# An audio-tower layer pair on one core: plain gathers with additions for six token tiles, adding gathers for six, and the causal mask written into PSUM by TensorE

## The chip, the cores and the metric

The kernel runs on one core of a Trainium2 chip. The metric is the device time of one execution in microseconds (us). The kernel before took 1510.72 us, the median of 3 runs (1509.34 to 1511.55). All times in the rows are us from the start of one profiled execution.

## The reference

64 sequences of 23 tokens (1472 tokens, 12 tiles of 128) pass through a token embedding and two layers:

```python
x -> tok:    layer_norm, x @ W, layer_norm                       # 1024 -> 512
L0 attention: power attention, 8 heads, gated                    # a = (q.k)**2 * exp(gate)
L0 ffn:      16 experts, top 4 of each token, plus a shared one  # h += sum of 4 expert rows
L1 attention: layer_norm, q (16 heads of 32), k, v (4 groups)
              rope, s = q.k / sqrt(32), causal softmax within each sequence, @ v, @ Wo, + h
L1 ffn:      quantized bit-linear feed-forward, + h
```

The change lies between the end of the L0 feed-forward and the end of the L1 attention.

## The kernel before

The program is written by hand for each engine, with semaphores between them; each engine runs its own list in order, so the order of the lists is the schedule. `h` holds the residual rows of all 12 tiles in SBUF.

The experts work on 61 tiles of slots. A token's row goes to four slots, and each slot's result is written to `yslot` in HBM (`keep`). When all are written, the four result rows of each token are added to `h`: `share(k, j)` (L502) is an indirect DMA issued by GpSimd that gathers, for the 128 tokens of tile `k`, the `j`-th row from `yslot` and adds it to `h` in flight. Each of the four of a tile waits by a semaphore until the one before it has landed. `shares(g, j)` issues the three of a group of three tiles. There are 48 in all. While the first run, TensorE still computes the last six tiles of the shared expert, whose result VectorE adds to `h` (L1738). Then VectorE and ScalarE prepare the weights of the next layer (`unit_a_lo`, `unit_b_lo`, L1395).

The L1 attention works in four chunks `c` of 16 sequences (368 tokens), which are not tile borders: chunk `c` needs the normalized tiles up to group `c` (three tiles each). For a group, VectorE takes statistics (`group_stats`, L1413, L1420), GpSimd the inverse root (`turned_root`, L466), VectorE the shift (`group_shift`, L1427); ScalarE normalizes (`normed`), TensorE turns the rows (`row_turn_l1`, L924), ScalarE and VectorE split the result into two half-precision parts (`high` L611, `low` L1432).

For a chunk, TensorE projects five blocks of queries and keys and one of values (`project`), into two PSUM banks in turn; ScalarE moves each out (`moved`, L786). VectorE shuffles (`rotate`, L1830), and the products with cosine and sine are shared out between VectorE (L1835) and GpSimd (`cosine`, L539, L541). VectorE sums them to `kr` and `qp` (`rotated`, L1844, L1845). TensorE forms the scores in PSUM banks 2 to 5 (L1255, 64 matmuls of float32, which the trace shows as 128). `centred` (L1848) is three passes of VectorE over 1472 columns: scores plus mask from PSUM into SBUF (L1852), row maximum (L1857), subtraction (L1858). After the first of them the banks are free (`f_cp`). ScalarE takes the exponential (L790), VectorE sums and scales (`weights`, L1864 to L1870), TensorE turns the weights (`turn`, L1265) and multiplies by the values (`weighted`, L1282, which writes the same banks 2 to 5), and ScalarE and VectorE split the result (`y_high` L803, `y_low` L1877). The turns of the rows for the next chunk stand between the projections in chunks 0 and 2, and after the weighted sums in chunk 1. The output projection and the second feed-forward follow (first row added at L1915).

## Time and profile before

| | |
|---|---|
| profiled execution | 1511.43 us, span 1509.5 us |
| TensorE busy | 1294.1 us (86%) |
| VectorE busy | 896.4 us (59%) |
| ScalarE busy | 629.5 us (42%) |
| GpSimd busy | 308.6 us (20%) |
| adding gathers (L506) | 48, mean 1684 ns, busy 80.8 us |
| chain of waits by line | L506 3%, L1255 2%, L539 1% of the span |

Busy shares are means over the whole span. In the stretch that the change touches no engine is full for long: GpSimd is, at first, and then the engines wait for each other in turn. A row of the timeline gives the start, the duration, engine, line and operation, and in brackets how long the engine sat idle before it and which instruction ended the wait; "issue" is time in which it waited for nothing that the profile shows.

### The profile page before, as it was taken

To read this page: it belongs to the slowest core of one execution; us is meant where nothing else is said; L and a number is where in the kernel's file an instruction comes from. 1 tells how busy PE (TensorE), PEld (TensorE's weight loads), DVE (VectorE), ACT (ScalarE), POOL (GpSimd) and SP (SyncE) were. 2 spreads that over 40 slices of the span, in tenths; PEclk is the share of its full clock that TensorE was granted. 3 is DMA by queue.
4 is the path that set the end of the run, shared out by engine and by line. 5 is a ranking of instruction groups with operands and counts; after the bars stand their busy time and mean duration, and the time that the engine had idled before them with its cause. 6 is when DMAs were issued, how large, how long until landed. Compare 5 with 4: busy or idle time off the path is not lost.

```text
span 1509.5 us, 30358 instructions
## 1 busy us (share of the span) xinstructions
PE 1294.1 (86%) x10660; PEld 829.6 (55%) x10674; DVE 896.4 (59%) x1865; ACT 629.5 (42%) x1066; POOL 308.6 (20%) x336
## 2 busy tenths in 40 slices
PE   6878899999999999986759999999972868768997
PEld 3446677777777877764424444444531656424443
DVE  5776455555565555668653555544332665578886
ACT  3445344444444444442314444444431333236664
POOL 2443000000000000000012233333267853010000
PEclk9997999999999999996779999999995869789999
DMA  5111343524435352422315767865268520000000
GB/s 181 68 66 43 100 178 138 200 105 174 142 127 204 135 185 109 156 85 89 124 70 178 257 227 257 303 242 170 98 125 133 85 43 3 2 1 8 21 21 32
DMA packets 44238, 184.26 MB, mean 122 GB/s; under 512 B 8688, under 2 KB 9200, under 8 KB 36368
## 3 DMA queue, kind: packets, MB, share of 16 engines
q0 software_dynamic: 21280, 95.41, 20.3%
q1 hardware_dynamic: 19440, 75.41, 14.3%
q10 hardware_dynamic: 3456, 12.58, 2.3%
q8 instruction: 42, 0.69, 0.2%
q14 instruction: 20, 0.16, 0.0%
HBM read 135.65 MB, written 47.73 MB: 121 GB/s over the span
## 4 chain that ended last, share of the span: by engine, by line
PE 55%; DVE 18%; issue 13%; POOL 7%; ACT 4%; DMA 2%; DVEq 1%; ACTq 0%; POOLq 0%; SPq 0%
PE ps L929 14%; PE ps L931 13%; PE ps L930 13%; POOL h L506 3%; PE ps L1036 3%; PE ps L1019 3%; PE ps L1255 2%; DVE ff L1976 2%; DVE amf L1983 1%; PE ps L1120 1%; PE ps L1052 1%; POOL rt_out L466 1%; PE ps L1348 1%; PE ps L1366 1%; POOL qraw L539 1%
## 5 line engine op out<-in xcount | busy, mean ns | idle before, releaser
L929 PE MATMUL ps<-nT_hi,wa_hi 128*128 128x368 f16 x448 | 147.9, 330 | 11.8 <-DVE wa_lo L1395 8.1
L930 PE MATMUL ps<-nT_lo,wa_hi 128*128 128x368 f16 x448 | 147.3, 329 | 0.0
L931 PE MATMUL ps<-nT_hi,wa_lo 128*128 128x368 f16 x448 | 147.0, 328 | 0.1
L496 POOL DMA_INDIRECT xg<-xrow,idx x61 | 61.4, 1007 | 276.7 <-PE ps L1120 121.5
L1559 DVE TENSOR_TENSOR a<-sq,E 92x368 f32<-92x368 f32 x64 | 31.7, 534 | 136.3 <-ACT sq L694 136.3
L1731 DVE SCALAR_TENSOR_TENSOR nrm<-ps,xg,nrm 128x256 f32<-128x256 f32 x61 | 29.5, 484 | 133.3 <-ACT nrm L737 112.1
L930 PE MATMUL ps<-wa_lo,nT_hi 128*92 128x128 f16 (+1 forms) x560 | 107.1, 235 | 0.0
L929 PE MATMUL ps<-wa_hi,nT_hi 128*92 128x128 f16 (+1 forms) x560 | 107.1, 235 | 0.0
L931 PE MATMUL ps<-wa_hi,nT_lo 128*92 128x128 f16 (+1 forms) x560 | 107.1, 235 | 0.0
L929 PE MATMUL ps<-wide,xT 128*128 x244 | 93.6, 383 | 12.9 <-issue 8.2
L491 POOL DMA_DIRECT2D wsp<-we_sp x16 | 8.6, 539 | 446.6 <-DVE we_sp L1395 446.6
L706 ACT ACTIVATE yT_hi<-ps 128x368 f16<-128x368 f32 x64 | 27.9, 475 | 164.9 <-PE ps L1052 164.9
L930 PE MATMUL ps<-wide,xT 128*128 x244 | 93.2, 382 | 0.0
L931 PE MATMUL ps<-wide,xT 128*128 x244 | 93.2, 382 | 0.0
L1533 DVE SCALAR_TENSOR_TENSOR wide<-ps,wide 128x368 f32<-128x368 f32 x128 | 69.1, 540 | 40.1 <-PE ps L931 40.1
L1348 PE MATMUL ps<-qw,qT 128*128 128x512 bf16 x372 | 86.5, 386 | 3.9 <-DVE ff L1976 2.6
L506 POOL DMA_INDIRECT h<-yslot,slot x48 | 80.8, 1684 | 15.4 <-issue 13.1
L929 PE MATMUL ps<-yT_hi,wb_hi 128*128 128x368 f16 x256 | 82.9, 324 | 1.2 <-DVE yT_lo L1581 1.2
L930 PE MATMUL ps<-yT_lo,wb_hi 128*128 128x368 f16 x256 | 82.8, 324 | 0.0
L931 PE MATMUL ps<-yT_hi,wb_lo 128*128 128x368 f16 x256 | 82.8, 324 | 0.0
L668 ACT ACTIVATE qk<-ps 128x368 f32<-128x368 f32 x96 | 45.1, 479 | 84.6 <-PE ps L931 84.5
L728 ACT ACTIVATE xT<-ps 128x1024 f16<-128x1024 f16 x61 | 62.3, 1022 | 28.9 <-PE ps L1120 22.0
(302 smaller groups left out, 3326.1 us busy)
## 6 DMA issues: line engine op xcount, KB each, us to landing
we_st<-in_we POOLq DMA_DIRECT2D x16, 1536.0 KB, 6.8
wsp<-we_sp POOLq DMA_DIRECT2D x16, 1536.0 KB, 5.4
wide<-wsp SPq DMA_DIRECT2D x16, 1536.0 KB
yslot<-yt POOLq DMA_DIRECT2D x61, 256.0 KB
wq_st<-in_ffq SPq DMA_DIRECT2D x24, 512.0 KB, 6.0
wq_st<-in_ffq ACTq DMA_DIRECT2D x24, 512.0 KB
wide<-in_wa SPq DMA_DIRECT2D x10, 1024.0 KB, 4.8
xt<-in_x SPq DMA_DIRECT2D x12, 512.0 KB, 3.5
```

The costliest lines, as they stand in the source:

```text
L496: pool.indirect_dma_start(Q["xg"][:, g % 4, :].bitcast(U32), None, xrow, bass.IndirectOffsetOnAxis(ap=idx[:, g:g + 1], axis=0)).then_inc(x ...
L506: pool.indirect_dma_start(h[:, k, :], None, yslot, bass.IndirectOffsetOnAxis(ap=slot[:, k, j:j + 1], axis=0), compute_op=ALU.add).then_inc ...
L668: nc.scalar.activation(B["qk"][:, j, :], ps[:, j % 2, 0:CW], ACT.Copy, scale=1.0 / WS).then_inc(b_ev, 1)
L728: nc.scalar.activation(Q["xT"][:, p].rearrange("p a b -> p (a b)"), ps[:, p, :].bitcast(F16), ACT.Copy).then_inc(m_xe, 1)
L929: nc.tensor.matmul(dst, lhs[0], rhs[0], start=start, stop=False)
L930: nc.tensor.matmul(dst, lhs[0], rhs[1], start=False, stop=False)
L931: return nc.tensor.matmul(dst, lhs[1], rhs[0], start=False, stop=stop)
L1019: ins = nc.tensor.matmul(ps[0:AT, 2 + j, a * REP * AT:(a + 1) * REP * AT], B["qk"][:, 2, tok], B["qk"][:, 0:2, tok], start=True, stop=True)
L1036: ins = nc.tensor.matmul(ps[0:AT, 4 + 2 * j + a, r * (DH + 1):(r + 1) * (DH + 1)], B["a"][0:AT, j, a, r, :], B["v1"][0:AT, 2 * j + a, :], ...
L1348: ins = nc.tensor.matmul(ps[:, 2 * (f % 2) + q, :], Gm["qT"][:, b, ds(k * P, P)], qw[:, q, b * FF + f * 512:b * FF + (f + 1) * 512], start ...
L1533: V.scalar_tensor_tensor(acc, ps[:, 6 + blk % 2, 0:CW], 1.0 / (WS * AS), acc, ALU.mult, ALU.add).then_inc(b_acc, 1)
L1559: V.tensor_tensor(B["a"][0:AT, j], B["sq"][0:AT, j], B["E"][0:AT, 2 * j:2 * j + 2].unsqueeze(2).broadcast_to([AT, 2, REP, AT]), ALU.mult). ...
```

## The change

Tiles 0 to 5 no longer use adding gathers. `collect(k)` issues four plain gathers into a landing buffer (three in the space of the expert weights, one in `wq_st`; tiles 4 and 5 reuse the buffers of tiles 0 and 1 and wait until these are read). VectorE adds the four rows and `h` with four additions (`returned`) ahead of the tile's statistics. Tiles 6 to 11 keep their adding gathers, at other places of GpSimd's list.

The mask becomes a bfloat16 tile `maskb` for 16 sequences. TensorE writes it into each of the four PSUM banks with one matmul by the identity, and the scores accumulate onto it. `centred` then has two passes, both reading PSUM: maximum and subtraction. The banks are free only after the subtraction (`f_sb`).

The order of the chunks is written alike for all: the turns of the next chunk's rows stand behind the scores, in chunk 0 ahead of them; the statistics of group `c + 1` stand behind the sums of chunk `c`; in chunks 1 to 3 the sine product of block 3 goes from GpSimd to VectorE.

```diff
+            def collect(k):
+                if k > 3:
+                    pool.wait_ge(c_h, ready(NT + k - 4))
+                for j in range(TOPK):
+                    pool.indirect_dma_start(landing[k][:, j, :], None, yslot,
+                                            bass.IndirectOffsetOnAxis(ap=slot[:, k, j:j + 1], axis=0)).then_inc(sh_in[k], 16)
...
-                if c and j < 4:
+                if c and j < 3:
                     nc.gpsimd.tensor_tensor(Fm["qs"][:, j, :], Fm["qs"][:, j, :], sinT[:], ALU.mult).then_inc(f_cos, 1)
-            for j in range(TOPK):
-                shares(0, j)
-                shares(1, j)
+            for k in range(5):
+                collect(k)
+            turned_root(0)
+            collect(5)
...
+            turned_root(2)
+            shares(3, 0)
+            shares(3, 1)
+            cosine(2, 0)
+            cosine(2, 1)
+            shares(3, 2)
+            cosine(2, 2)
+            shares(3, 3)
+            cosine(2, 3)
+            cosine(2, 4)
+            turned_root(3)
...
@@ TensorE, scores @@
+                for g in range(G4):
+                    nc.tensor.matmul(ps[:, 2 + g, 0:CW], identb[:], maskb[:], start=True, stop=False)
...
-                                               Fm["kr"][d, s * SL:(s + 1) * SL], start=True, stop=True)
+                                               Fm["kr"][d, s * SL:(s + 1) * SL], start=False, stop=s == 15)
@@ TensorE, weighted @@
-                    pe.wait_ge(f_cp, c + 2)
+                    pe.wait_ge(f_sb, c + 2)
@@ TensorE, chunks @@
                 for j in range(2, 6):
                     project(c, j)
-                    if c % 2 == 0 and j < 5:
-                        row_turn_l1(k + j - 2)
                 if c:
                     turn(c - 1)
+                    scores(c)
+                    weighted(c - 1)
+                if c + 1 < CH:
+                    for j in range(GT):
+                        row_turn_l1(k + j)
                 if c == 0:
+                    scores(c)
+                if c + 1 < CH:
                     project(c + 1, 0)
                     project(c + 1, 1)
...
@@ VectorE @@
+            def returned(k):
+                y = landing[k]
+                dve.wait_ge(sh_in[k], SHARES[k] + 64)
+                dve.sem_inc(passed, 1)
+                V.tensor_tensor(y[:, 0, :], y[:, 0, :], y[:, 1, :], ALU.add)
+                order(V.tensor_tensor(y[:, 2, :], y[:, 2, :], y[:, 3, :], ALU.add))
+                order(V.tensor_tensor(row(k), row(k), y[:, 0, :], ALU.add))
+                V.tensor_tensor(row(k), row(k), y[:, 2, :], ALU.add).then_inc(c_h, 1)
...
+            V.tensor_copy(maskb[:].rearrange("p (h s) -> p h s", s=SL), mask1[:].unsqueeze(1).broadcast_to([P, 16, SL])).then_inc(f_mk, 1)
             group_stats(0)
             group_shift(0)
-            group_stats(1)
...
+            rotate(0, 0)
+            rotate(0, 1)
+            group_stats(1)
+            dve.wait_ge(wa_hi, UNITS + 1)
+            split_lo(wo[1][:].rearrange("p a b -> p (a b)"), st_a[:], wo[0][:].rearrange("p a b -> p (a b)"), wa_lo)
             for c in range(CH):
                 k = GT * (c + 1)
-                rotate(c, 0)
-                rotate(c, 1)
                 if c:
+                    rotate(c, 0)
+                    rotate(c, 1)
                     weights(c - 1)
                 for j in range(2, 5):
-                    if c % 2 == 0:
-                        low(k + j - 2)
                     rotate(c, j)
+                if c == 0:
+                    group_shift(1)
                 rotated(c)
...
+                if 0 < c < CH - 1:
+                    group_stats(c + 1)
+                    group_shift(c + 1)
                 if c:
+                    centred(c)
                     y_low(c - 1)
-                if c == 1:
+                if c + 1 < CH:
                     for j in range(GT):
                         low(k + j)
```

GpSimd, from the last write of the expert results to the first roots of the attention, before (`h<-yslot` is an adding gather of one tile, `rt_out` the root of one group):

```order
L500 DMA yslot<-yt 128x512 x6
L506 DMA h<-yslot,slot 128x512 x27
L466 TENSOR_TENSOR rt_out<-rt_in,neg_half 128x3
L549 MEMSET qp 128x64x9
L506 DMA h<-yslot,slot 128x512 x3
L466 TENSOR_TENSOR rt_out<-rt_in,neg_half 128x3
```

The same place in the changed kernel (`wide<-yslot` and `wq_st<-yslot` are plain gathers into landing buffers):

```order
L504 DMA yslot<-yt 128x512 x6
L510 DMA wide<-yslot,slot 128x512 x12
L510 DMA wq_st<-yslot,slot 128x512 x4
L510 DMA wide<-yslot,slot 128x512 x4
L470 TENSOR_TENSOR rt_out<-rt_in,neg_half 128x3
L510 DMA wide<-yslot,slot 128x512 x4
L516 DMA h<-yslot,slot 128x512 x3
L549 TENSOR_TENSOR qraw<-qraw,cosT 128x368 x2
L561 MEMSET qp 128x64x9
```

Thirty adding gathers stood ahead of the root of group 1 and 27 ahead of that of group 0; now 20 plain ones stand ahead of the root of group 0, and the adding gathers of group 2 begin behind it.

GpSimd at chunk 2, before (the root at the end of the first three lines is that of group 3, the products are those of chunk 2's five blocks):

```order
L506 DMA h<-yslot,slot 128x512 x3
L466 TENSOR_TENSOR rt_out<-rt_in,neg_half 128x3
L506 DMA h<-yslot,slot 128x512 x3
L466 TENSOR_TENSOR rt_out<-rt_in,neg_half 128x3
L539 TENSOR_TENSOR qraw<-qraw,cosT 128x368
L541 TENSOR_TENSOR qs<-qs,sinT 128x368
L539 TENSOR_TENSOR qraw<-qraw,cosT 128x368
L541 TENSOR_TENSOR qs<-qs,sinT 128x368
L539 TENSOR_TENSOR qraw<-qraw,cosT 128x368
L541 TENSOR_TENSOR qs<-qs,sinT 128x368
```

The same place in the changed kernel:

```order
L516 DMA h<-yslot,slot 128x512 x6
L549 TENSOR_TENSOR qraw<-qraw,cosT 128x368
L551 TENSOR_TENSOR qs<-qs,sinT 128x368
L549 TENSOR_TENSOR qraw<-qraw,cosT 128x368
L551 TENSOR_TENSOR qs<-qs,sinT 128x368
L516 DMA h<-yslot,slot 128x512 x3
L549 TENSOR_TENSOR qraw<-qraw,cosT 128x368
L551 TENSOR_TENSOR qs<-qs,sinT 128x368
L516 DMA h<-yslot,slot 128x512 x3
L549 TENSOR_TENSOR qraw<-qraw,cosT 128x368 x2
L470 TENSOR_TENSOR rt_out<-rt_in,neg_half 128x3
```

Before, all gathers were out ahead of chunk 2's products; now six of them stand between these products.

VectorE, from the centring of chunk 2 to the first shuffles of chunk 3, before:

```order
L1852 TENSOR_TENSOR wide<-ps,mask 128x1472
L1857 TENSOR_REDUCE mx<-wide 128x64
L1858 TENSOR_TENSOR wide<-wide,mx 128x1472
L1877 TENSOR_TENSOR nT_lo<-ps,nT_hi 128x4x4x23 x4
L1830 STREAM_SHUFFLE qs<-qraw 128x368 x2
```

The same place in the changed kernel:

```order
L1868 TENSOR_REDUCE mx<-ps 128x64
L1869 TENSOR_TENSOR wide<-ps,mx 128x1472
L1889 TENSOR_TENSOR nT_lo<-ps,nT_hi 128x4x4x23 x4
L1432 TENSOR_TENSOR nT_lo<-ps,nT_hi 128x4x128 x3
L1844 STREAM_SHUFFLE qs<-qraw 128x368 x2
```

A pass of the centring is gone, and the three low halves of the next chunk's rows (`L1432`) stand between the centring and chunk 3; before, they stood between the shuffles of chunk 2.

TensorE after the scores of chunk 2, before (only the first of the projection's matmuls are shown):

```order
L1265 MATMUL ps<-ident,wide 128x128 x16
L1255 MATMUL ps<-kr,qp 128x23 x64
L929 MATMUL ps<-nT_hi,wa_hi 128x368
L930 MATMUL ps<-nT_lo,wa_hi 128x368
L931 MATMUL ps<-nT_hi,wa_lo 128x368
```

The same place in the changed kernel:

```order
L1270 MATMUL ps<-ident,wide 128x128 x16
L1256 MATMUL ps<-maskb,identb 128x368 x4
L1260 MATMUL ps<-kr,qp 128x23 x64
L1287 MATMUL ps<-wide,V 32x92 x64
L925 MATMUL ps<-ident,nrm 128x128 x12
L930 MATMUL ps<-nT_hi,wa_hi 128x368
```

The weighted sums and the twelve matmuls that turn three row tiles now stand between the scores and the first projection of chunk 3.

## Rows read from the trace of the kernel before

**Rows 1.** Busy time by stage; columns: us, then each engine busy (instructions), PEclk, DMA share, GB/s.

```profile
1104.00:1158.00 54.00, 18.81 (x101) 8.74 (x99) 14.25 (x27) 9.86 (x17) 45.57 (x29) 0.73 0.89 147
...
1308.00:1509.50 201.50, 172.84 (x933) 82.54 (x944) 162.48 (x360) 101.75 (x205) 16.39 (x26) 0.96 0.04 15
```

**Rows 2.** GpSimd in order of time, plain gather: start us, us, engine line op.

```profile
787.84 0.95 POOL L496 DMA_INDIRECT xg<-xrow,idx  x1 [0.30 <-issue]
```

**Rows 3.** GpSimd in order of time, around the adding gathers.

```profile
1138.13 1.55 POOL L506 DMA_INDIRECT h<-yslot,slot  x1 [0.30 <-issue]
...
1168.32 0.96 POOL L539 TENSOR_TENSOR qraw<-qraw,cosT 128x368 f32<-128x368 f32 x1 [4.05 <-DVE qs L1830]
...
1241.66 0.96 POOL L541 TENSOR_TENSOR qs<-qs,sinT 128x368 f32<-128x368 f32 x1
```

**Rows 4.** VectorE in order of time, shared tiles to the first shift.

```profile
1104.94 0.68 DVE L1738 SCALAR_TENSOR_TENSOR h<-ps,h 128x512 f32<-128x512 f32 x1
...
1127.07 1.22 DVE L1395 SCALAR_TENSOR_TENSOR wb_lo<-wide,wb_hi 128x1024 f16<-128x1024 f32 x1
...
1145.61 0.70 DVE L1413 BATCH_NORM_STATS2 bst<-h 128x6 f32<-128x512 f32 x1 [17.33 <-issue]
...
1157.29 0.16 DVE L1427 SCALAR_TENSOR_TENSOR nb<-mv,rt_out 128x3 f32<-128x3 f32 x1 [6.51 <-POOL rt_out L466]
```

**Rows 5.** VectorE in order of time: root answered, ordered successor, products, output weights.

```profile
1167.67 0.57 DVE L1830 STREAM_SHUFFLE qs<-qraw 128x368 f32<-128x368 f32 x1
...
1168.39 1.28 DVE L1835 TENSOR_TENSOR qs<-qs,sinT 128x368 f32<-128x368 f32 x1 [0.15 <-DVE qs L1830]
...
1186.61 2.29 DVE L1395 SCALAR_TENSOR_TENSOR wo_lo<-wide,wo_hi 128x2048 f16<-128x2048 f32 x1
...
1236.24 0.16 DVE L1427 SCALAR_TENSOR_TENSOR nb<-mv,rt_out 128x3 f32<-128x3 f32 x1 [0.99 <-POOL rt_out L466]
...
1311.50 0.18 DVE L1922 BATCH_NORM_AGGREGATE mv<-bst 128x2 f32<-128x6 f32 x1 [0.15 <-DVE bst L1920]
```

**Rows 6.** VectorE in order of time: chunk starts, centring ends, stage end.

```profile
1198.93 0.56 DVE L1830 STREAM_SHUFFLE qs<-qraw 128x368 f32<-128x368 f32 x1
...
1237.50 0.57 DVE L1830 STREAM_SHUFFLE qs<-qraw 128x368 f32<-128x368 f32 x1
...
1261.53 1.69 DVE L1858 TENSOR_TENSOR wide<-wide,mx 128x1472 f32<-128x1472 f32 x1
...
1293.54 1.89 DVE L1877 TENSOR_TENSOR nT_lo<-ps,nT_hi 128x368 f16<-128x368 f32 x4 [1.87 <-ACT nT_hi L803]
...
1307.47 0.69 DVE L1915 SCALAR_TENSOR_TENSOR h<-ps,h 128x512 f32<-128x512 f32 x1 [0.29 <-PE ps L931]
```

**Rows 7.** The chain of waits in order of time: start us, us, what.

```profile
1186.75 6.98 PE ps L1255 x128
...
1197.31 1.70 DVE wide L1858
...
1213.50 7.08 PE ps L1255 x128
...
1224.16 1.70 DVE wide L1858
...
1233.41 0.31 PE ps L930
...
1252.89 5.03 PE ps L1255 x128
...
1267.83 0.58 DVE qs L1830 x2
...
1280.80 5.60 PE ps L1255 x128
...
1289.98 1.70 DVE wide L1858
```

**Rows 8.** TensorE in order of time: weighted sums of chunk 0.

```profile
1222.39 2.33 PE L1282 MATMUL ps<-wide,V 32*32 32x92 f32 x128 [1.86 <-issue]
```

More of the change, by code:

```diff
@@ L209, in build @@
         xn = flat.rearrange("p (k d) -> p k d", d=D)
+        landing = [flat[:, 2048 * x:2048 * x + 2048].rearrange("p (j d) -> p j d", d=D) for x in range(3)]
+        landing += [wq_st[:].rearrange("p a b -> p (a b)")[:, 0:2048].rearrange("p (j d) -> p j d", d=D), landing[0], landing[1]]
         fT = nT[0][:].rearrange("p a b -> p (a b)")[:, 0:2 * FF].bitcast(BF16).rearrange("p (x a b) -> p x a b", x=2, b=P)
@@ L851, in _ @@
                     moved(c + 1, 0)
+                if c == 0:
+                    exponential(c)
+                if c + 1 < CH:
                     moved(c + 1, 1)
[L853 to L859 removed]
             weights_turned(CH - 1)
```

118 lines of the change are left out of this document (42 added, 76 removed).

## The prediction

> **What bounds the kernel now.** I read the windows by stage first. Between 1104 and 1158 us GpSimd is busy 45.57 of 54 us while TensorE, VectorE and ScalarE do little, and this is where the rows computed by the experts return to h; everything after 1308 us is not touched by the change [rows 1]. So the part that can move is 1104 to 1308 us, and I follow it by one marker, the start of each chunk (its first shuffle), and compare the same marker before and after.
>
> GpSimd in order of time shows what the front costs: an adding gather holds the engine 1.55 us and the next follows 0.30 later, so one every 1.85 [rows 3]. Tile 0's last addition is the 19th, issued at 1138.13; VectorE reads the tile at 1145.61, 7.5 us later [rows 3, 4]. Three more gathers (tiles 6 to 8) stand in GpSimd's queue ahead of the root, so VectorE's first shift is at 1157.29 after waiting 6.51 us for it [rows 4]. From there the chain goes through four chunks: products on VectorE and GpSimd, scores on TensorE (6.98, 7.08, 5.03, 5.60 us), centring on VectorE, and round again [rows 7]. Chunks start at 1167.67, 1198.93, 1237.50, 1267.83; the stage ends at 1307.47, the first output row [rows 5, 6, 7]. The steps are 31.3, 38.6, 30.3 and 39.6 us. The second step is long because the rows of chunk 2 are normalized and turned after chunk 1's centring: 1224.16 + 1.70 = 1225.86 to 1237.50 is 11.6 us. The third is short because the turns of chunk 3 stand between chunk 2's projections: 1261.53 + 1.69 = 1263.22 to 1267.83 is 4.6 us [rows 6, 7].
>
> **The change, part by part.**
>
> *Front.* A plain gather costs 0.95 + 0.30, 1.25 us [rows 2]. Sixteen are out by 1104.4 + 20 = 1124.5, beside the shared tiles; tile 4 must wait for tile 0's landing buffer. VectorE is free at 1127.07 + 1.22 = 1128.3 [rows 4]. The mask copy (368 columns) has no row: between 0.2 and 1.2, I take 0.5, near the 0.57 of a 368-wide shuffle [rows 5]. Then each tile needs four 512-wide additions. None with both inputs in SBUF is in the trace: a 512-wide one with an input in PSUM took 0.68 [rows 4]; a 368-wide product beside a GpSimd product took 1.28 [rows 5]. I take 0.68. The second, third and their successors wait in order, 0.15 after the end of the one before [rows 5]: 0.60 + 0.83 + 0.83 + 0.70 for the four, and 0.65 for the statistics, 3.6 per tile. Three tiles end at 1139.6, the aggregates at 1140.3, and the root takes 1.0 (the wait of 0.99) [rows 5], so the first shift is at 1141.3 instead of 1157.3: **16.0 ahead**. GpSimd's tile 4 gathers run 1131.8 to 1136.8 and are hidden by VectorE; if additions cost only 0.54, they would still be.
>
> *Chunk 0.* The way from the shift to the first shuffle is unchanged, 10.4 us: 1151.7. Two rotations take 3.2, then VectorE takes the additions of tiles 3 to 5 (10.8 + 0.7), which before it did not do at all, then the low half of the output weights, 2.29 [rows 5], three rotations 3.7 and the two sums of 368 and 1472 columns 2.2. That gives 1174.6 for the queries. Before, scores began at 1186.75 [rows 7]: 12.1 ahead. Then the three row turns of chunk 1, earlier spread between the projections, stand ahead of the scores: 1.9 us until the third turn is done, at 1176.5. The four mask matmuls have 368 columns; the trace has a 368-column matmul every 0.31 us at the lower clock [rows 7], and half that is the bound if the clock is full. I take 1.2. Scores, 7.0: 1184.7, 9.0 ahead. Centring loses one pass of 1472 columns (1.69 + 0.15) of three, so it takes 3.5 instead of 5.3: 1188.2 against 1197.31 + 1.70 = 1199.0, 10.8 ahead. The first projection of chunk 1 now follows the scores (12 times 0.31, 3.7, then 0.6 for the copy): chunk 1 starts at 1189.0, 9.9 ahead.
>
> *Chunk 1.* On GpSimd tile additions shares(2, 3) now stand between the products of the second and third column block. From the chunk's start: 0.65, four products of 0.93, three gathers of 1.85, four products, the two sums 2.1: 15.8 us, 1204.8. Before, scores began at 1213.50: 8.7 ahead. Masks 1.2, scores 7.1: 1213.1; centring 3.5: 1216.7 against 1225.86, 9.2 ahead. The weighted sums now wait for the subtraction, since the scores stay in PSUM until then; before they ran inside the centring, at 1222.39 [rows 8]. So the way to the next marker is 11.6 + 1.0 (2.33 for the sums and 0.5 for the first copy, against the 1.87 that the exponential and that copy took [rows 6]): chunk 2 starts at 1229.3, 8.2 ahead.
>
> *Chunk 2.* GpSimd's first four products end 5.1 after the chunk's start (1241.66 + 0.96 against 1237.50 [rows 3, 6]): 1234.4. Then three gathers 5.55, two products 1.9, three gathers 5.55, two products 1.9, the sums 2.1: 1251.4. Before, scores began at 1252.89: only 1.5 ahead. TensorE has nothing to do in between, so I price the scores at 7.0 and the masks at 1.2 where before the scores took 5.03: 1259.6. Centring: 1263.1 against 1263.22, **level**. Now comes the step that I think decides: the turns of chunk 3's rows, their low halves and its first projection follow the centring, 12.6 us, where 4.6 stood before. Chunk 3 starts at 1275.7 against 1267.83: **7.9 behind**.
>
> *Chunk 3.* 13.0 to the scores, 1288.7; masks 0.6 with TensorE just busy, scores 5.6: 1294.9; centring 1298.4 against 1289.98 + 1.70 = 1291.68, 6.7 behind; the low halves of chunk 2's results start after the weighted sums, 2.9 instead of 1.87: **7.8 behind** to the end.
>
> The product moved from GpSimd to VectorE in each later chunk (one of 0.93) is in these sums. The profiled execution took 1511.43 with a span of 1509.5; with 7.8 it becomes 1519.2. The median is 0.7 lower; the steps are rounded, and small collisions of products that the old trace has are left out of the new walk. I forecast **1519**.
>
> **A rule on the shared port.** A 368-wide product of VectorE took 1.28 us while GpSimd worked on one of its own from 1168.32 [rows 3, 5]. The Trainium skill, page "SBUF — State Buffer", section "Who interferes with whom", says that a VectorE instruction with two SBUF inputs and a GpSimd instruction that reads SBUF exclude each other for a whole instruction; by that rule the row agrees, and the new additions, which have two SBUF inputs, would be the ones that suffer. What it would make of the sum is the second rival.
>
> **The rivals.**
>
> *The lead is not spent in chunk 2 (other side).* If GpSimd's gathers of shares(3, 2) and (3, 3) do not hold back the products behind them, because a product can run while the gather ahead of it is still being issued, the 11.1 us leave chunk 2: centring ends at 1252.0 and chunk 3 starts at 1264.6, 3.2 ahead; with chunk 3's masks and late sums the end is 3.3 ahead, 1508. For it speaks that spans of GpSimd instructions overlap in the trace; against it that 0.30 + 1.55 lies between starts of gathers throughout, and that in chunk 0 the wait for the products already grew where gathers stood between them. It decides if the third cosine of chunk 2 starts before 1237. Chance 0.14 (two thirds of it faster).
>
> *The additions collide.* If each of the 11 additions that can meet GpSimd work takes 1.28 instead of 0.68, 6.6 more: 1526. For it speaks the product of 1.28; against it that GpSimd has little to read while VectorE adds. Chance 0.15.
>
> *A lower price of the turns.* If TensorE holds the higher clock through chunks 2 and 3 (masks 0.6 and not 1.2, scores 5.0 and not 7.0, projections at half of 3.7), 1.2 + 2.0 + 1.9 come back, 1514. Chance 0.12; of this a part lies within 0.2%.
>
> The forecast's own case has 0.59, with 1515 to 1525.
>
> **How the numbers follow.** The bounds: 24 additions at 0.54 each are 3.4 less, at 1.28 each 14.4 more; masks 2.5 to 4.9 against 4.2 taken; the mask copy 0.3 less or 0.7 more. The range runs from the other side's 1508, rounded up, to where about half of the 14.4 is used: 1509 to 1531. A measurement of this kernel tells some 0.2%, 3 us, from no change. Faster than 1507.7 to slower than 1513.7: faster 0.12 (the first rival and mistakes in the walk), within 0.11 (what is left of the first, part of the third), slower 0.77.
>
> **What would show it.** Right: first shift near 1141, chunk starts near 1152, 1189, 1229 and 1276, six adding gathers between products of chunk 2 with TensorE idle, and more than 11 us between chunk 2's subtraction and chunk 3's first shuffle. Wrong: a first shift after 1146 (additions over 0.9 each), or chunk 3 starting before 1268.

## The result and the profile after

The changed kernel took 1535.3 us, the median of 4 runs (1533.12 to 1537.33), against 1511.13 us before (4 runs): a ratio of 1.0161 with a 95% interval of 1.0143 to 1.0179. It is 24 us slower. I had forecast 1519 us with a range up to 1531 us, so the direction was right and the size was not.

The windows by stage, columns as in [rows 1], show that the part behind the marker is the same (202 us, with TensorE busy for 175.0 against 172.8) and that the loss lies before it. The middle row is a stretch in which almost nothing runs but GpSimd's gathers:

```profile
1104.00:1158.00 54.00, 25.53 (x115) 11.95 (x113) 23.08 (x41) 12.84 (x22) 24.16 (x25) 0.76 0.42 127
...
1116.00:1119.00 3.00, 0.96 (x5) 0.22 (x3) 0.00 (x0) 0.00 (x0) 2.09 (x3) 1.00 0.71 220
...
1331.60:1533.60 202.00, 174.98 (x948) 82.76 (x946) 162.99 (x360) 101.86 (x205) 16.46 (x26) 0.96 0.04 15
```

The same three microseconds of the kernel before, whose adding gathers are under way:

```profile
1116.00:1119.00 3.00, 3.00 (x18) 1.50 (x17) 1.45 (x3) 1.00 (x2) 2.68 (x2) 1.00 0.89 126
```

TensorE is busy 3.00 of 3.00 us before and 0.96 after, though the DMA engines are busier before (0.89 against 0.71). They move less before, though: 126 GB/s against 220.

VectorE after, in order of time, answers to [rows 4 to 6]. The last part of the slots' work ends at 1139.98 + 1.22 = 1141.2 us, 12.9 later than before; then come the additions, the first shift (1153.58), the four chunk starts (the shuffles L1844) and the end marker (1331.58):

```profile
1139.98 1.22 DVE L1395 SCALAR_TENSOR_TENSOR wb_lo<-wide,wb_hi 128x1024 f16<-128x1024 f32 x1
1141.12 0.34 DVE L1834 CAST maskb<-mask 128x368 bf16<-128x368 f32 x1
1141.38 0.69 DVE L1800 TENSOR_TENSOR wide<-wide 128x512 f32<-128x512 f32 x1
...
1153.58 0.16 DVE L1427 SCALAR_TENSOR_TENSOR nb<-mv,rt_out 128x3 f32<-128x3 f32 x1 [1.00 <-POOL rt_out L470]
...
1164.26 0.56 DVE L1844 STREAM_SHUFFLE qs<-qraw 128x368 f32<-128x368 f32 x1
...
1203.29 0.57 DVE L1844 STREAM_SHUFFLE qs<-qraw 128x368 f32<-128x368 f32 x1
...
1213.16 5.37 DVE L1849 TENSOR_TENSOR qs<-qs,sinT 128x368 f32<-128x368 f32 x1
...
1245.97 0.57 DVE L1844 STREAM_SHUFFLE qs<-qraw 128x368 f32<-128x368 f32 x1
...
1277.60 1.69 DVE L1869 TENSOR_TENSOR wide<-ps,mx 128x1472 f32<-128x1472 f32 x1
...
1291.60 0.57 DVE L1844 STREAM_SHUFFLE qs<-qraw 128x368 f32<-128x368 f32 x1
...
1331.58 0.69 DVE L1928 SCALAR_TENSOR_TENSOR h<-ps,h 128x512 f32<-128x512 f32 x1 [0.29 <-PE ps L932]
```

The end marker is 24.1 us behind [rows 6]. From the first shift on it takes 178.0 us, where before it took 1307.47 - 1157.29 = 150.2. I had forecast the first shift at 1141.3 and the end marker at 1315.3: of the 16.3 us that are missing, 12.3 are there at the first shift, and 4.0 come in the chunks.

What happened between 1105 and 1141 us stands in three views. ScalarE in order of time waits 7.24 and 5.03 us, and the profile finds no instruction that ended these waits ("remote"):

```profile
1113.38 0.38 ACT L753 ACTIVATE nrm<-ps 128x256 f32<-128x256 f32 x1 [2.07 <-PE ps L932]
...
1121.92 0.60 ACT L748 ACTIVATE hT<-ps 128x512 f16<-128x512 f16 x1 [7.24 <-remote]
1127.55 0.38 ACT L753 ACTIVATE nrm<-ps 128x256 f32<-128x256 f32 x1 [5.03 <-remote]
```

TensorE in order of time had done the products that ScalarE waits for. The four transposes of the first wait start at 1115.28, the last product of the second at 1116.58; then TensorE itself waits for ScalarE:

```profile
1115.28 0.38 PE L1138 MATMUL ps<-identh,hh 128*128 128x128 f16 x4 [0.72 <-DVE hh L1734]
...
1116.58 0.38 PE L932 MATMUL ps<-wa_hi,nT_lo 128*128 128x512 f16 x1
1122.66 0.59 PE L930 MATMUL ps<-wb_hi,hT 128*128 128x512 f16 x1 [5.70 <-issue]
```

The chain of waits puts both gaps down to "another core or an unknown queue". Its last two rows are used further down:

```profile
1114.68 7.22 another core or an unknown queue
...
1121.94 5.58 another core or an unknown queue
...
1232.23 2.63 PE ps L1287 x106
...
1259.89 5.68 DMA h<-yslot,slot
```

The trace also records when each semaphore count arrives, which no view of the profile prints. I compared the modelled end of each product of TensorE that counts a semaphore with that arrival:

```
product (changed kernel)              modelled end   count arrives   late by
gate and up, tile a    (L932)            1111.97        1113.36        1.39
down projection        (L932)            1113.26        1114.82        1.56
transposes of hh       (L1138)           1115.66        1121.90        6.23
gate and up, tile b    (L932)            1116.96        1127.52       10.56
down projection        (L932)            1125.38        1127.60        2.22
transposes of hh       (L1138)           1130.03        1130.04        0.01
```

(One more, at 1110.67, has no arrival in the trace; ScalarE goes on at 1110.71.) In the kernel before all 15 such counts between 1104 and 1130 us come 0.01 to 0.02 us after the end. So ScalarE was not slow: TensorE's counts reached it 1.4 to 10.6 us late, from seven microseconds into the burst of sixteen plain gathers until the last of them had landed (near 1127 us). Counts of ScalarE and VectorE in the same stretch come on time (median 0.01 us). The additions into `h` stand every 4.1 us before; here three steps are 5.5, 14.2 and 5.1 us, 12.4 us more in sum. Half a microsecond of offset between the two traces is there already at 1105 us.

The gathers do not pile up meanwhile. By their landing counts, as far as these are in the trace, each plain gather of the burst lands 3.0 to 3.6 us after its start, the last (1123.87) no later than the first, so two or three are under way at a time. An adding gather takes 4.7 to 5.8 us in the kernel before, at one every 1.88: about as many are under way there. What sets the burst apart is its pace, one gather every 1.27 us. One more thing goes with it. A landing is told by 16 counts, and of the 256 of these sixteen gathers the trace holds only 65; in the kernel before it holds 155 of 176.

### The profile page after: what moved, and what is told of

Same layout as the page of the kernel before. It is cut to its first block, busy times and chain, and to the rows that moved or that the text cites. A ratio compares the mean times of both kernels' runs of the same rounds, so it can differ in the third digit from the quotient of the medians.

```text
span 1533.6 us, 30430 instructions
## 1 busy us (share of the span) xinstructions
PE 1309.9 (85%) x10689; PEld 835.4 (54%) x10690; DVE 913.8 (60%) x1889; ACT 630.8 (41%) x1066; POOL 288.2 (19%) x333
## 4 chain that ended last, share of the span: by engine, by line
PE 58%; DVE 19%; issue 12%; ACT 4%; POOL 3%; DMA 2%; DVEq 1%; another core or an unknown queue 1%; ACTq 0%; POOLq 0%; SPq 0%
PE ps L930 15%; PE ps L932 14%; PE ps L931 14%; PE ps L1037 3%; PE ps L1020 3%; PE ps L1260 2%; DVE ff L1989 2%; PE ps L1121 1%; DVE amf L1996 1%; PE ps L1053 1%; POOL rt_out L470 1%; PE ps L1366 1%; PE ps L1348 1%; PE ps L1138 1%; DVE bst L1465 1%
## 5 line engine op out<-in xcount | busy, mean ns | idle before, releaser
L932 PEld LDWEIGHTS ps<-wa_hi,nT_lo 128*92 128x92 f16 (+1 forms) x560 | 67.7, 121 | 7.4 <-issue 3.0
```

The lines of the kernel that those rows point to most:

```text
L932: return nc.tensor.matmul(dst, lhs[1], rhs[0], start=False, stop=stop)
```

## The experiments

Times are medians; ratios are against the kernel before on the same chip. The experiments ran on four chips (e1 to e4, e5 to e8, e9 to e12, and e13 with e14), on which the kernel before took 1510.1 to 1511.5 us, so a difference of medians between runs of two chips can be off by a microsecond or two; where it matters, the difference by the ratios is given too. "Shift to end" is the time from the first shift to the end marker, in one traced execution of each kernel, which can lie up to 5 us from the median (e11 1510.9, e7 1508.8).

| run | what it is | us | ratio [95%] | first shift | shift to end |
|---|---|---|---|---|---|
| before | | 1511.1 | 1 | 1157.3 | 150.2 |
| after | | 1535.3 | 1.0161 [1.0143, 1.0179] | 1153.6 | 178.0 |
| e1 | gathers behind the shared tiles | 1538.0 | 1.0174 [1.0157, 1.0191] | 1152.9 | 179.9 |
| e2 | gathers spaced, two under way | 1525.0 | 1.0083 [1.0067, 1.0100] | 1143.9 | 180.2 |
| e3 | ScalarE's code moved | 1535.0 | 1.0153 [1.0136, 1.0170] | 1152.6 | 178.4 |
| e4 | plain gathers alone | 1515.8 | 1.0030 [1.0019, 1.0042] | 1152.1 | 158.8 |
| e5 | order alone | 1522.8 | 1.0081 [1.0064, 1.0099] | 1152.7 | 166.5 |
| e6 | mask alone | 1512.2 | 1.0011 [1.0001, 1.0021] | 1157.0 | 149.3 |
| e7 | e4, two under way | 1504.1 | 0.9954 [0.9939, 0.9969] | 1142.2 | 162.4 |
| e8 | e2, mixed order | 1510.8 | 1.0004 [0.9995, 1.0013] | 1141.9 | 164.9 |
| e9 | e2, old mask | 1521.4 | 1.0067 [1.0052, 1.0082] | 1142.9 | 175.5 |
| e10 | e2, pieces ahead of products | 1516.3 | 1.0040 [1.0027, 1.0053] | 1140.8 | 169.5 |
| e11 | old order, two kinds of gathers | 1505.8 | 0.9966 [0.9952, 0.9980] | 1152.5 | 152.4 |
| e12 | burst of eight | 1527.5 | 1.0111 [1.0095, 1.0126] | 1144.3 | 179.8 |
| e13 | mixed order, two kinds | 1505.4 | 0.9966 [0.9953, 0.9979] | 1146.1 | 156.2 |
| e14 | old order, same front as e13 | 1504.7 | 0.9951 [0.9933, 0.9969] | 1148.2 | 153.9 |

**Is the standstill made by the gathers? (e1 to e3, e12)** I first took it for a standstill of ScalarE; that TensorE's counts are what is late I found in the traces afterwards, before e12.

```diff
+            pool.wait_ge(m_y, VT)                      # e1
             for k in range(5):
                 collect(k)
```

> The changed kernel with one more wait: GpSimd sends the plain gathers only when the last shared tile is through the slots' down projection, so that none is under way while the shared tiles still run. Theory A (the stretch of 12.4 us in which ScalarE stands still, 1114.7 to 1127.5 us, is made by plain gathers that move at their full rate beside it): the stretch goes, the last part of the slots' work ends near 1129 us instead of 1141, the gathers run from about 1126 to 1146 us and the shift of the first group is out near 1148 us instead of 1153.6; end 1529 to 1531 us. Theory B (it belongs to the place of the code or to the landing place of something else, and not to the gathers): the stretch stays, the gathers start later behind it, and the end is 1540 us or more.

The additions into `h` are back to one every 4.1 us and no count is late, as A has it. But the end did not follow: 1538.0 us, outside the ranges of both theories. Tile 2 lands only at 1144.5, the root of the group is asked for at 1148.7, and GpSimd answers at 1152.0, since tile 4's four gathers stand ahead of the root. I had left those out of my 1148.

```diff
-            for k in range(5):                         # e2
-                collect(k)
+            for g in range(2):
+                for j in range(TOPK):
+                    for k in (2 * g, 2 * g + 1):
+                        if j:
+                            pool.wait_ge(sh_in[k], SHARES[k] + 16 * j)
+                        plain gather (k, j)
+            collect(4)
```

> The changed kernel with the 16 plain gathers of tiles 0 to 3 sent in pairs of tiles, a piece of a tile only when the piece before it of the same tile has landed, so that at most two are under way. Theory A in its first form (a backlog of plain gathers holds ScalarE up): no stretch without work at 1114.7 to 1127.5 us, the last part of the slots' work ends near 1129 us, the shift of the first group is out at 1141 to 1145 us, the end is 1523 to 1527 us. Theory A in its second form (any plain gather at this time does it, whatever the backlog): the stretch stays 10 us or longer, the end is 1533 to 1540 us.

1525.0 us, 10.3 less than the changed kernel (11.8 by the ratios), and every count whose arrival is in the trace is 0.01 to 0.02 us behind its product (two arrivals are missing; what waits for them starts on time). ScalarE in order of time keeps the old step of 4.1 us:

```profile
1116.49 0.60 ACT L754 ACTIVATE hT<-ps 128x512 f16<-128x512 f16 x1 [1.52 <-PE ps L1144]
...
1120.60 0.60 ACT L754 ACTIVATE hT<-ps 128x512 f16<-128x512 f16 x1 [1.52 <-issue]
```

The gathers go to the same landing buffers as in the changed kernel, so the landing place alone does not make counts late. Their mean pace is one every 1.71 us.

```diff
+            for n in range(40):                        # e3, ScalarE
+                act.wait_ge(m_gu, 1)
             for v in range(SF + 1 + 4 * LOOPS, VT + 1):
```

> The changed kernel with 40 semaphore waits that are already met put in ahead of ScalarE's instructions for the last shared tiles, which moves all that follows them in its program by 40 instructions and costs under 1.5 us by itself. Theory C (ScalarE stands still because its next piece of program is being fetched beside the gathers, at the place where a fetch falls): the standstill moves to another instruction, or shrinks, and its length changes by 3 us or more. Theory A (it is held up by the gathers whatever it runs): ScalarE stands still over the same time, until the gathers end near 1127 us, and the end stays within 2 us of 1535.

The end stayed (1535.0 us), and counts are again late by 1.5, 3.7, 9.1 and 10.6 us, the last one arriving at 1127.96. One instruction transfer in the trace carries 16 KB, and a shift of 40 instructions may be too small against it, so this alone would not exclude code fetching. The transfers speak against it: one starts at 1113.1 us in the changed kernel and the next at 1153.3, but one starts at 1112.8 in the kernel before and at 1113.0 in e2 just so, and there no count is late.

```diff
+            collect(0)                                 # e12
+            collect(1)
+            pool.wait_ge(m_y, VT)
-            for k in range(5):
+            for k in range(2, 5):
                 collect(k)
```

> The changed kernel with only tiles 0 and 1 (eight plain gathers, back to back) sent beside the shared tiles; those of tiles 2 and 3 wait until the last shared tile is through the slots' down projection. In the changed kernel TensorE's semaphore counts arrive 1.4 to 10.6 us late, from 1112 us (seven microseconds into the burst) until the last of the sixteen has landed. Theory A (the delay grows with the backlog): counts are late by under 3 us and only until 1117 us, the last part of the slots' work ends near 1131 us; tiles 2 and 3 come late, the first shift near 1146 us, the end 1526 to 1530 us. If a burst holds them up whatever its length: 5 us or more late, and the end is 1532 us or more.

Counts are late by 1.5, 1.5 and 0.3 us, the last at 1115.3, and then on time. 1527.5 us, as the first case has it. But the reason in that case, a backlog, is not what the trace shows: these gathers too land 3.1 to 3.6 us after their start. The delay grows with the length of the burst at this pace. All runs by the mean pace of the gathers that start before 1124 us:

```
run                        one gather every   landing counts in the trace   TensorE's counts
before, e5, e6             1.88 us, adding     88 to 97%                     on time
e2, e7, e8, e9, e10        1.71 to 1.74       79 to 86%                     on time
e11                        1.52               83%                           on time
e13, e14                   1.40, 1.43         34, 30%                       up to 2.1 us late
e12                        1.27 (eight)       38%                           1.5 us late
after, e3, e4              1.26 to 1.27       22 to 25%                     up to 10.6 us late
```

Pace, number under way and GB/s (119 to 191 in e2's windows of 3 us, 197 to 220 in the changed kernel's) move together in these runs, so it is not shown which of them matters.

**The three parts apart (e4 to e7).** Each of e4 to e6 is one part of the change on the kernel before:

```diff
-            for j in range(TOPK):                      # e4, and `returned` ahead of the statistics
-                shares(0, j)
-                shares(1, j)
+            for k in range(5):
+                collect(k)
+            turned_root(0)
+            collect(5)
...
+            rotate(0, 1)                               # e5: all lists in the changed order,
+            group_stats(1)                             # with adding gathers and the mask pass
...
+                for g in range(G4):                    # e6, and the centring in two passes
+                    nc.tensor.matmul(ps[:, 2 + g, 0:CW], identb[:], maskb[:], start=True, stop=False)
```

> The kernel before with the plain gathers and their additions alone, the order of the chunks and the mask as before. Theory A: the standstill of 10 to 13 us near 1115 to 1127 us is there too; the shift of the first group is out near 1153.6 us, 3.7 us ahead of before; in the old order that lead is mostly kept or lost to the six tiles' additions on VectorE; end 1508 to 1515 us. If the standstill came from the new order or from the mask: the shift is out near 1142 us and the end is 1498 to 1505 us.

> The kernel before with the order of the changed kernel alone (first chunk's rotation split by the second group's statistics, all row turns behind the scores of their chunk, GpSimd's products and pieces interleaved as after), adding gathers and the old mask pass kept. Theory D (the new order is the loss: from the first group's shift to the end of the attention it takes 178 us where the old takes 150): the first shift is out at 1152 to 1154 us, because its root no longer stands behind three gathers, and the end is 1532 to 1538 us, though neither plain gathers nor the standstill of ScalarE are there. Theory E (the loss is in the additions and the mask on TensorE): 1512 to 1520 us.

> The kernel before with the mask written into PSUM by four products of TensorE ahead of the scores, and the centring in two passes instead of three; nothing else changed. Each chunk pays 0.8 to 1.4 us of TensorE ahead of its scores and gets 1.8 to 1.9 us of VectorE back behind them. If the chain runs through both, the end is 1 to 2 us earlier: 1508.5 to 1511 us. If the masks at the low clock cost as much as the pass, or the chain runs past the centring, no change within 1 us of 1511.3. If the writes into PSUM slow the scores, later: 1513 us and more.

e4: 1515.8 us, 0.8 above the range forecast. The late counts are there without the new order and without the mask (1.4, 9.1 and 10.6 us). The lead of 5.2 us at the shift became a lag of 4.7 at chunk 0 (1172.37 against 1167.67 [rows 5]). VectorE in order of time shows why: the second group's twelve additions stand ahead of what chunk 0 needs:

```profile
1152.13 0.16 DVE L1435 SCALAR_TENSOR_TENSOR nb<-mv,rt_out 128x3 f32<-128x3 f32 x1 [1.00 <-POOL rt_out L468]
...
1163.15 0.69 DVE L1421 BATCH_NORM_STATS2 bst<-h 128x6 f32<-128x512 f32 x1
...
1172.37 0.56 DVE L1852 STREAM_SHUFFLE qs<-qraw 128x368 f32<-128x368 f32 x1
```

e5: neither of my two forecasts. The order alone costs 11.6 us, not the 24 of D, and the 178 us that I carried over from the changed kernel are 166.5. VectorE's rows of first and second shift and of the end, first of e5, then of e2, tell where the rest is:

```profile
1152.70 0.16 DVE L1414 SCALAR_TENSOR_TENSOR nb<-mv,rt_out 128x3 f32<-128x3 f32 x1 [1.01 <-POOL rt_out L467]
...
1176.61 0.91 DVE L1414 SCALAR_TENSOR_TENSOR nb<-mv,rt_out 128x3 f32<-128x3 f32 x1
...
1319.24 0.69 DVE L1902 SCALAR_TENSOR_TENSOR h<-ps,h 128x512 f32<-128x512 f32 x1 [0.29 <-PE ps L923]
```

```profile
1143.94 0.16 DVE L1433 SCALAR_TENSOR_TENSOR nb<-mv,rt_out 128x3 f32<-128x3 f32 x1 [1.00 <-POOL rt_out L470]
...
1176.53 0.91 DVE L1433 SCALAR_TENSOR_TENSOR nb<-mv,rt_out 128x3 f32<-128x3 f32 x1
...
1238.05 0.57 DVE L1850 STREAM_SHUFFLE qs<-qraw 128x368 f32<-128x368 f32 x1
...
1324.10 0.69 DVE L1934 SCALAR_TENSOR_TENSOR h<-ps,h 128x512 f32<-128x512 f32 x1 [0.29 <-PE ps L938]
```

With plain gathers the first shift is 8.8 us earlier, the second is not earlier at all: the head start goes into the additions of tiles 3 to 5 (three times 2.9 us). The other 4.9 us in these two traces come later, and e9 asks for them.

e6: 1.0 us more (interval 0.01 to 0.21%), as forecast in the middle case; its one trace has the end marker 1.1 us earlier. The mask part brings nothing in the old order.

> The plain gathers alone in the old order, but at most two of them under way as in the second experiment. Theory A: no standstill of ScalarE; the first shift is out at 1143 to 1145 us instead of 1152.1 with the backlog, and as chunk 0 starts 20 us behind it in the old order, it starts near 1164 us and the end is 1505 to 1510 us. If the old order can't use an early first group (its chunk 0 waits for the second group's statistics): the end stays at 1513 to 1517 us.

e7 (e4 with the loop of e2) is 1504.1 us, 7.0 less than before and 11.7 less than e4 (11.5 by the ratios), and 0.9 less than the range forecast. It beats both kernels. VectorE in order of time: first shift, chunk 0, end.

```profile
1142.22 0.16 DVE L1441 SCALAR_TENSOR_TENSOR nb<-mv,rt_out 128x3 f32<-128x3 f32 x1 [1.00 <-POOL rt_out L468]
...
1162.57 0.57 DVE L1858 STREAM_SHUFFLE qs<-qraw 128x368 f32<-128x368 f32 x1
...
1304.59 0.69 DVE L1943 SCALAR_TENSOR_TENSOR h<-ps,h 128x512 f32<-128x512 f32 x1 [0.20 <-PE ps L945]
```

**The order taken apart (e8 to e10).** e9 is e2 with the old mask (the four products, `maskb` and the two-pass centring taken out again). e8 moves group 3 back and gives the sine product of block 3 back to GpSimd, e10 moves only the pieces (the adding gathers of group 3):

```diff
+                    if c == 2:                         # e8, VectorE; TensorE and ScalarE alike
+                        low(k + j - 2)
                     rotate(c, j)
+                if c == 1:
+                    group_stats(3)
+                    group_shift(3)
...
-            cosine(2, 0)                               # e10, GpSimd
-            cosine(2, 1)
             shares(3, 2)
-            cosine(2, 2)
             shares(3, 3)
-            cosine(2, 3)
-            cosine(2, 4)
+            for j in range(5):
+                cosine(2, j)
```

> The second experiment (changed kernel, plain gathers at most two under way) with the old mask pass on VectorE instead of the four products of TensorE. Theory F (in the new order the mask on TensorE is a loss, because the scores' banks come free only after both passes of the centring, 3.4 us later than after the mask pass, and the weighted sums, the row turns and the next chunk's projections stand behind that): chunk 2 starts about 11.5 us after chunk 1's centring instead of 13.8, the scores start 1.2 us earlier in each chunk, the end is 1520 to 1523 us against 1525.0. Theory G (the mask on TensorE is worth its pass in either order): 1526 to 1529 us.

Shift to end falls from 180.2 to 175.5 us in the traces; in the medians the difference is 3.6 us, by the ratios 2.4, and the two intervals overlap. So the times alone do not settle it: that the mask costs something in the new order rests on one trace each, and on the order of the steps in them. The chain of waits of e9 goes through ScalarE behind the subtraction of chunk 1, because the weighted sums were done inside the centring:

```profile
1221.73 1.43 ACT wide L811
1223.16 0.39 ACT nT_hi L824
```

In the changed kernel the same place is 1232.23, 2.63, PE L1287, then the copy: the sums stand behind the subtraction. Chunk 2 starts 11.5 us after the centring in e9 (1233.25 against 1221.7) and 13.8 in the changed kernel.

> The second experiment with the six adding gathers of group 3 that stood between GpSimd's products of chunk 2 put ahead of the first of them. As forecast, a product in GpSimd's queue waits for the gathers ahead of it: they then run in the 11 us in which GpSimd idled before chunk 2, the way from chunk 2's start to its sum of the keys falls from 19.7 to 13 to 15 us, and the end is 1519 to 1521 us against 1525.0. If the products did not wait for them, no change: 1524 to 1526 us.

8.7 us less than e2 (6.5 by the ratios, as the two ran on different chips), more than I had thought: from chunk 2's start to the sum of the keys it takes 11.6 us, where I had 13 to 15. GpSimd in order of time now ends the pieces as the chunk starts, and VectorE has its chunk 2 and 3 starts at:

```profile
1234.69 1.54 POOL L516 DMA_INDIRECT h<-yslot,slot  x1 [0.38 <-DMA h<-yslot,slot]
1235.67 1.55 POOL L549 TENSOR_TENSOR qraw<-qraw,cosT 128x368 f32<-128x368 f32 x1
```

```profile
1234.88 0.57 DVE L1847 STREAM_SHUFFLE qs<-qraw 128x368 f32<-128x368 f32 x1
...
1269.93 0.57 DVE L1847 STREAM_SHUFFLE qs<-qraw 128x368 f32<-128x368 f32 x1
```

Chunk 2 to chunk 3 is 35.0 us instead of 45.6.

> Gathers paced as in the second experiment, mask on TensorE, the new order for chunk 0 and chunk 1's scores, and the old order for group 3: its statistics and shift in chunk 1, its row turns between the projections of chunk 2, GpSimd's pieces of groups 2 and 3 ahead of chunk 2's products. Theory D: chunk 0 starts near 1155 us, chunk 1 near 1194.6 us (4.3 us ahead of before), chunks 1 to 3 take the old 108.6 us, end 1305 us to 1505 and 1509 us for the whole. If the loss of the new order lies in chunks 0 and 1 and not in where group 3 stands: 1518 us and more.

e8 puts group 3's statistics, shift and row turns back in their old places, as well as the pieces. 1510.8 us: no different from before, 2 us above the range. Chunk 0 (1152.7) and chunk 1 (1191.6) are ahead, but from chunk 1 to chunk 2 it takes 44.3 us instead of 38.6: one round of pieces is still between chunk 1's products (1197.4 to 1201.1), and the weighted sums wait for the subtraction. How the 5.7 us divide between these was not tried alone.

**Two kinds of gathers (e11, e13, e14).** Plain gathers for tiles 0 to 2 only, adding gathers for 3 to 5, so that VectorE has 12 additions and not 24.

```diff
+            for k, j in ORDER:   # e13, e14: (0,j) (1,j) (2,j), then one of tiles 3 to 5
+                (collect if k < GT else share)(k, j)
```

> The kernel before (old order, old mask pass) with plain gathers for the first group of three tiles only, each sent with an adding gather of the second group near it, so that no two tiles' plain gathers pile up, and the first root ahead of the third group's pieces. Theory: plain gathers bring the first group forward, while the second group's additions on VectorE (10.4 us, what held chunk 0 up by 20 us behind the first shift in the seventh experiment) are not needed, since its sums are made by the transfers. First shift at 1142 to 1144 us, chunk 0 10.4 us behind it at 1153 to 1155, the old steps of 31, 39, 30 and 40 us after it, if groups 2 and 3 are in time: 1497 to 1502 us. If TensorE's late semaphores come back with any plain gather, or group 3's pieces come late: 1503 to 1509 us.

> The mixed order of the eighth experiment with the old mask pass, plain gathers for the first group only (three tiles in turn, an adding gather of the second group after each round), adding gathers for the second group, GpSimd's products of a chunk never parted by pieces. If the causes found so far add up (standstill gone, second group's additions off VectorE, mask off TensorE, pieces ahead of products): first shift near 1141 us, chunk 0 near 1151.5, chunk 1 near 1186, then the old steps, 1497 to 1501 us. If three plain gathers under way hold up TensorE's semaphores, or the second group is late for chunk 0 (its last piece goes out near 1142 us and lands near 1149): 1502 to 1508 us.

> The same front in the old order of all chunks. There chunk 0 waits for the second group's statistics, which wait for its adding gathers (last one out near 1142 us, landed near 1149): first shift near 1141 us, second near 1152, chunk 0 near 1155, the old steps after it: 1498 to 1502 us. If TensorE's counts are late again under three plain gathers: 1504 us or more. Against e13 it tells whether the new chunk 0, freed of its costs, is worth anything over the old one.

e11 gains 0.34%, but its first shift is out at 1152.5 and not at 1143: GpSimd stood in line for landings (4.28 us at once near 1137) and tile 2 landed at 1145. That trace is the slowest of its five executions, 5.1 us above their median, so part of this may be its own. e13 and e14 both carry late counts again, graded: 0.2 to 2.1 us, with three plain gathers and an adding one sent in turn; their last slots' work ends at 1132.3 and 1135.1 instead of 1128.3. The new chunk 0 (e13) is 2.0 us ahead at chunk 1 and level at chunk 2, as VectorE's rows of the two starts show, first e13, then e14:

```profile
1191.74 0.56 DVE L1846 STREAM_SHUFFLE qs<-qraw 128x368 f32<-128x368 f32 x1
...
1232.16 0.57 DVE L1846 STREAM_SHUFFLE qs<-qraw 128x368 f32<-128x368 f32 x1
```

```profile
1193.72 0.56 DVE L1851 STREAM_SHUFFLE qs<-qraw 128x368 f32<-128x368 f32 x1
...
1232.29 0.57 DVE L1851 STREAM_SHUFFLE qs<-qraw 128x368 f32<-128x368 f32 x1
```

So the new chunk 0 brings nothing over the old that can be told. All three missed the range of their first case, by 2.7 to 4.4 us, and fell into that of the second, which had named late counts or late pieces. In e13 and e14 counts were late; in e11 none was, and it was tile 2 that landed late. The rest was lost in chunk 1. e7, e13 and e14 can't be told apart.

## Why the prediction was wrong

**The step that failed** is the first of the front: "Sixteen are out by 1104.4 + 20 = 1124.5, beside the shared tiles". The gathers were out on time (1104.88, spacing 1.26, last at 1123.87), but I priced "beside" at nothing. It cost 12.4 us in the trace and 10.3 (e2) to 11.7 us (e7 against e4) in the medians, of 16.3 us by which the forecast was short. In its place the runs show TensorE's counts arriving up to 10.6 us late beside the burst, so that the last shared tiles end late, and with them the slots' work on VectorE (12.9 us in the trace, 0.5 of it the offset). No rival and no bound of mine held a way in which a transfer slows an engine that shares no buffer with it, so the range stopped 4 us short.

**The rest of the front was right.** Additions took 0.69 (I took 0.68), a tile 3.48 (3.6), the mask copy 0.34 (0.5), and from the start of the first addition to the first shift 12.2 us passed (12.5). The plain gathers kept the price of [rows 2]. The rival of colliding additions is out: none of the 24 took more than 0.69. My sign of a wrong front, a first shift after 1146, did come (1153.6), but the reason that I had put behind it, additions over 0.9 each, was not there.

**The chunks were right in kind, short in sum.** Forecast and measured distances, us:

| | shift to chunk 0 | 0 to 1 | 1 to 2 | 2 to 3 | 3 to end | sum |
|---|---|---|---|---|---|---|
| forecast | 10.4 | 37.3 | 40.3 | 46.4 | 39.6 | 174.0 |
| after | 10.7 | 39.0 | 42.7 | 45.6 | 40.0 | 178.0 |

In chunk 0 the scores start 3.6 us after the sums, where I had 3.1, and the sums come 1.0 later. In chunk 1 one sine product on VectorE took 5.37 us; it began at 1213.16, and four GpSimd products followed one another from 1213.81 to 1218.1. GpSimd in order of time: the first plain gather, two of these products, and a piece with the product behind it in chunk 2:

```profile
1104.88 1.00 POOL L510 DMA_INDIRECT wide<-yslot,slot  x1 [2.01 <-DMA yslot<-yt]
...
1213.81 1.57 POOL L549 TENSOR_TENSOR qraw<-qraw,cosT 128x368 f32<-128x368 f32 x1
1214.73 1.57 POOL L551 TENSOR_TENSOR qs<-qs,sinT 128x368 f32<-128x368 f32 x1
...
1254.29 1.54 POOL L516 DMA_INDIRECT h<-yslot,slot  x1 [0.30 <-issue]
1255.28 1.55 POOL L549 TENSOR_TENSOR qraw<-qraw,cosT 128x368 f32<-128x368 f32 x1
```

I had priced GpSimd's products at 0.93 each and left "small collisions of products" out; with this one the sums of chunk 1 came 1.6 us later than forecast, and the weighted sums (1232.23 to 1235.64, 3.4 us and not 2.33) put another 1.1 behind the centring. The Trainium skill, page "SBUF — State Buffer", section "Who interferes with whom", has the rule for it: two SBUF inputs on VectorE and a GpSimd instruction that reads SBUF exclude each other for a whole instruction. The trace agrees, and adds that VectorE got no turn between four GpSimd products: its product ends 0.4 us behind the last of them. In chunk 2 the same happened again, over a piece and two products, where VectorE had time to spare. GpSimd's spans are rough; by them VectorE's product began 0.65 us ahead of the first of the four, though it takes 0.54 alone.

```profile
1254.75 3.40 DVE L1849 TENSOR_TENSOR qs<-qs,sinT 128x368 f32<-128x368 f32 x1
```

**Which step decided.** I named the turns of chunk 3 behind the centring (12.6 us forecast, 12.3 measured). The forecast of the distance was right. But the pieces between chunk 2's products weigh as much: the last two rows of GpSimd's fence above show a product that starts only 1.0 us after the third piece has started, and the chain row 1259.89 is 5.68 us behind pieces; putting them ahead gave 8.7 us (e10; 6.5 by the ratios). The rival "the lead is not spent in chunk 2" is out by the same rows: products did wait for the pieces, though only for the first 1.0 us of the last of three, where I had taken 1.85. The rival of the higher clock held for chunk 3 alone (4.14 us for its scores; 6.97 in each of the others).

**The sum of the parts.** Order alone 11.6 (e5), late counts 10.3 (e2), mask in the new order about 3.6 to 4.7 (e9), paced plain gathers in the new order -1.4 (e9 against e5): 24.1 to 25.2, measured 24.2. The agreement proves nothing: before, e5, e9, e2 and after are one chain of kernels, and the differences of its links must add up to the whole; only 4.7, the trace's value for the mask, is from outside it. Each link also holds only at its place in the chain, and e9 against e5 is within the noise. In the old order the paced gathers alone bring 7.0.

**Open** is by what path plain gathers at a fast pace delay TensorE's counts. The ends of products are modelled, so the trace doesn't tell whether the products' writes or the counts alone were late. Nor is it told whether the data or the 16 counts of each landing are what crowds them. In the six kernels with late counts the trace also lacks most of the landing counts (22 to 38% are in it), and in e1, whose gathers run at one every 1.41 us when TensorE's shared tiles are done, it holds 74%. So the recording of the trace may have a part in the delay itself; no run here tells the two apart.

## What to carry to other kernels

Price a burst of transfers not only by queue and buffer: put it beside running products in one experiment, and look at when counts arrive; if they come late, space the transfers out. Here waiting for the landing before last was enough. An engine that is free early is worth only what the next thing in its list needs: here the second group's additions took what the first group's gathers gave. A reordering should be run alone. GpSimd's transfers belonged ahead of its products, in its idle time, and not between them (e10). And parts that are measured along one chain of kernels always add up; a sum is a check only if a part is measured outside the chain.

## What the runs showed of the hardware

- Beside plain gathers of 128 rows of 2 KB, TensorE's semaphore counts arrive late: by nothing at one gather every 1.71 us (e2, e7), 1.5 us with eight at one every 1.27 (e12), up to 2.1 us with three plain and one adding in turn at one every 1.4 (e13, e14), up to 10.6 us in a burst of sixteen at one every 1.27 (after, e3, e4). With adding gathers alone, one every 1.88 (before, e5), never, though the DMA engines' share was higher (0.89 against 0.71). Counts of ScalarE and VectorE were not late. The Trainium skill, page "SBUF — State Buffer", section "Who interferes with whom", says that a DMA never contends with a compute engine and that PE never waits for anyone. It speaks of access to SBUF, and the products in the burst are shown with their 0.38 us as elsewhere; but what TensorE hands on did come late beside the gathers.
- In the stretch behind the late counts the granted clock fell to 0.56 (1122 to 1125 us), so 1.2 GHz for most of it, after TensorE had stood still for 5.7 us.
- A plain gather landed 3.0 to 3.6 us after its start in the burst (after), an adding one 4.7 to 5.8 (before).
- A VectorE product with two SBUF inputs took 5.37 us beside four GpSimd products, and 3.40 beside a gather's issue and two products, where the same took 0.54 undisturbed (after).
